# Two of eight tile pairs of a final weighted sum computed by GpSimd instead of VectorE

## What is computed

```python
x = x + 0.5 * ffn(layernorm(x))      # first expert layer
x = x + attention(layernorm(x))
x = x + 0.5 * ffn(layernorm(x))      # second expert layer

# in ffn: each token goes to the best 4 of 16 experts
vals, idx = top_k(logits, 4)
gates_k = softmax(vals)
y = einsum('emi,edi->emd', act, w2) + b2
delta = einsum('me,emd->md', G, y)   # G holds the 4 gates of a token
return x + delta
```

## Time and profile before

| | us |
|---|---|
| median of 3 runs | 1039.29 |
| lowest, highest | 1039.18, 1043.13 |
| the profiled execution | 1044.55 |
| its span | 1042.8 |
| its last stage, from the last indirect DMA at 1003.98 | 38.8 |

### The profile page before, as it was taken

One profiled execution on the slowest core, in us unless ns is written; L12 is line 12 of the kernel. 1 busy time (PEld: TensorE's weight loads), 2 busy tenths in 40 slices (PEclk: granted clock), 3 DMA queues, 4 the chain that ended last, 5 costly groups with the idle time before them and its releaser, 6 DMA issues.

```text
span 1042.8 us, 22336 instructions
## 1 busy us (share of the span) xinstructions
PE 712.3 (68%) x5722; PEld 427.6 (41%) x5722; DVE 610.4 (59%) x1961; ACT 445.8 (43%) x974; POOL 328.5 (32%) x356
## 2 busy tenths in 40 slices
PE   2222079999999926767788297287209999999930
PEld 1111046555665613223343143144106666666620
DVE  6776335555555555677787268237405566666547
ACT  2533035555555524336556135142005555555520
POOL 3667613333333313101111500503532333333320
PEclk9999999999999977869999699698559999999985
DMA  9654334555445344622212313325232333333338
GB/s 306 252 207 160 121 104 130 167 167 164 149 126 138 89 134 129 199 73 72 79 32 59 122 39 101 118 83 180 105 119 82 90 92 95 95 92 94 85 121 282
DMA packets 120111, 131.63 MB, mean 126 GB/s; under 512 B 39596, under 2 KB 101525, under 8 KB 119864
## 3 DMA queue, kind: packets, MB, share of 16 engines
q1 hardware_dynamic: 101656, 91.11, 29.3%
q0 software_dynamic: 13728, 34.64, 9.3%
q10 hardware_dynamic: 4608, 4.46, 1.2%
HBM read 69.54 MB, written 64.21 MB: 128 GB/s over the span
## 4 chain that ended last, share of the span: by engine, by line
PE 46%; DVE 12%; issue 11%; SPq 10%; ACT 7%; another core or an unknown queue 5%; DMA 4%; ACTq 4%; POOL 0%; DVEq 0%; POOLq 0%
PE banks L406 15%; PE banks L428 7%; ACT w2s L1438 4%; PE banks L1233 3%; PE banks L415 3%; PE banks L388 2%; PE banks L402 2%; PE banks L1278 2%; PE banks L1211 2%; SPq L218 2%; DVE X L726 2%; DVE X L1545 2%; SPq L231 2%; SPq L217 2%
## 5 line engine op out<-in xcount | busy, mean ns | idle before, releaser
L340 POOL DMA_INDIRECT y_rows<-y,goal x158 | 155.4, 984 | 333.5 <-ACT y L498 318.4
L406 PE MATMUL banks<-w1s,rT 128*128 x948 | 233.7, 383 | 0.0
L688 DVE TENSOR_SCALAR pbh<-banks 128x256 f32<-128x256 f32 x158 | 67.1, 425 | 199.7 <-ACT pbh L484 128.7
L1603 DVE CUSTOM_DVE_ANT_0 pbh<-banks,maskq 128x128 bf16<-128x128 f32 (+3 forms) x256 | 113.2, 487 | 69.8 <-PE banks L1188 46.3
L1438 ACT ACTIVATE w2s<-banks 128x1024 f32<-128x1024 f32 (+3 forms) x128 | 89.6, 700 | 138.1 <-PE banks L1219 98.6
L406 PEld LDWEIGHTS banks<-w1s,rT 128*128 128x128 f16 x948 | 93.6, 99 | 96.4 <-issue 4.0
L428 PE MATMUL banks<-w2s,hsT 128*128 x948 | 129.2, 273 | 0.0
L484 ACT ACTIVATE pbh<-banks 128x256 f32<-128x256 f32 x158 | 60.5, 383 | 125.2 <-PE banks L406 118.6
L477 ACT ACTIVATE rT<-banks 128x512 f16<-128x512 f16 x158 | 93.5, 592 | 42.7 <-issue 35.5
L1125 POOL DMA_INDIRECT x_rows<-row,row_to x64 | 61.8, 965 | 132.0 <-DVE row_to L1736 113.7
L491 ACT ACTIVATE hsT<-pbh 128x256 f16<-128x256 f32 x158 | 65.8, 416 | 72.1 <-DVE pbh L696 49.2
(11 more groups left out here) (238 smaller groups left out, 1077.9 us busy)
## 6 DMA issues: line engine op xcount, KB each, us to landing
row<-x_rows SPq DMA_DIRECT2D x158, 128.0 KB
arena<-in_w SPq DMA_DIRECT2D x16, 512.0 KB, 7.5
w1s<-y_rows SPq DMA_DIRECT2D x16, 512.0 KB, 5.0
arena<-y_rows SPq DMA_DIRECT2D x16, 512.0 KB, 7.8
qk_split<-w1s SPq DMA_DIRECT2D x48, 128.0 KB
arena<-qk_split SPq DMA_DIRECT2D x64, 96.0 KB, 2.3
w_lent<-w1s SPq DMA_DIRECT2D x22, 256.0 KB
w1s<-w_lent SPq DMA_DIRECT2D x11, 512.0 KB
```

What stands on the lines that cost most here:

```text
L340: pool.indirect_dma_start(y_rows[m], bass.IndirectOffsetOnAxis(ap=goal[:, c, :], axis=0), y[:, n % NY, :], None, bounds_check=K * T - 1, o ...
L406: mm = pe.matmul(o, rT[:, n % 2, 2 * r + k, :], w1s[:, bass.ds(e, 1), k, w, :], start=False, stop=(k == HC - 1 and w == 1))
L1603: dve.tensor_tensor_reduce(junk[:, (n * U + j) % 3, 0:W], query_bank[j % 4][:, 0:W], maskq[:, SEQ - W:], 1.0, -3e38, ALU.add, ALU.max, mx[ ...
```

## The change

Pairs 2 and 5 are summed by GpSimd. [...] Each addition waits for its multiplication. The semaphore `pool_summed` counts these instructions, 16 for a pair. They stand in GpSimd's program behind the last indirect DMA. VectorE sums pairs 0, 1, 3, 4, 6 and 7. The semaphore `combined` goes; SyncE waits for the count of sums of whichever engine has the pair. SyncE's order of loads and stores stays.

```diff
+            BY_POOL = (2, 5)
+            BY_DVE = tuple(j for j in range(NT // 2) if j not in BY_POOL)
...
+                def wait_combined(j):
+                    if j in BY_POOL:
+                        sp.wait_ge(ev("pool_summed"), (BY_POOL.index(j) + 1) * K * 2 * 2)
+                    else:
+                        sp.wait_ge(ev("summed"), (BY_DVE.index(j) + 1) * K * 2)
...
                 def store_out(j):
-                    sp.wait_ge(ev("combined"), j + 1)
+                    wait_combined(j)
...
                         if i >= NB:
-                            sp.wait_ge(ev("combined"), (i - NB) // 2 + 1)
+                            wait_combined((i - NB) // 2)
                         load_back(i)
...
+                for j in BY_POOL if m == 1 else ():
+                    for k in range(K):
+                        for t in range(2):
+                            i, done = 2 * j + t, BY_POOL.index(j) * K * 2 + 2 * k + t
+                            if k == 0:
+                                pool.wait_ge(y_back[i % NB], i // NB * 16 + 16)
+                            pool.tensor_scalar(back[:, i % NB, k, :], back[:, i % NB, k, :], gate[:, i, k:k + 1], None,
+                                               ALU.mult).then_inc(ev("pool_summed"), 1)
+                            pool.wait_ge(ev("pool_summed"), 2 * done + 1)
+                            if k == 0:
+                                pool.wait_ge(ev("residual"), i + 1)
+                            pool.tensor_tensor(X[:, i, :], X[:, i, :], back[:, i % NB, k, :], ALU.add)\
+                                .then_inc(ev("pool_summed"), 1)
...
-                                dve.wait_ge(ev("summed"), (j * K + k - 1) * 2 + t + 1)
+                                dve.wait_ge(ev("summed"), (BY_DVE.index(j) * K + k - 1) * 2 + t + 1)
...
-                    dve.wait_ge(ev("summed"), (j + 1) * K * 2)
-                    dve.sem_inc(ev("combined"), 1)
...
-                for j in range(NT // 2 if m == 1 else 0):
+                for j in BY_DVE if m == 1 else ():
                     combine(j)
```

## The result

The changed kernel takes 1053.64 us (median of 4 runs, 1048.99 to 1057.25) against 1039.24 us: a ratio of 1.0133, 95% interval 1.0077 to 1.0190. A second series gave 1.0117 (1.0070 to 1.0164). It is slower, as forecast, but by 14 us where 5.7 were forecast, and it lies above the range, whose top was 1052.

What follows compares the result with a forecast made beforehand. The prediction took VectorE's sums to bound the last stage, with the loads 0.5 us behind. VectorE's end 5.4 us later plus 0.3 us of stores gave +5.7 us on the median 1039.29, so 1045.0 us; range 1040.5 to 1052.

Steps and rivals of the forecast that it cites:

- The bound and what could be had: Last stage: VectorE ends last, loads close behind; of 8.1 us taken off VectorE at most 0.5 to 0.8 reach the end.
- the slack: Last token tile's load: said to land at 1035.0, wanted by VectorE at 1035.45, so 0.5 us to spare.
- The exclusion: VectorE's sums and GpSimd's instructions reading SBUF wait for each other; 10.6 us put on VectorE for 8.1 taken off.
- unit: One GpSimd multiplication and the addition waiting for it, 16 in all: 1.29 us alone, 1.67 us beside VectorE.
- the same rule: VectorE loses the length of the GpSimd instruction less 0.26 us: 0.47 to an addition, 0.19 to a multiplication.
- The multiplication: GpSimd's multiplication by a pointer scalar, not in the trace: taken as 0.45 us, between 0.30 and 0.73.
- SyncE's queue: Loads 12 and 13 wait for GpSimd's pair 2, with later loads and stores behind them; out about 8 us later.
- The timetable: Last stage event by event: GpSimd's pair 2 ends at 1029.5, pair 5 at 1042.9, VectorE at 1044.1, 5.4 us later.
- Rival 3: Longer GpSimd units: 1.95 us gives +9.7 (1049), 1.98 gives +11.2 (1050.5), both together +15 us; chance 0.17.
- The sum: Whole change: VectorE ends 5.4 us later, the bunched last stores add 0.3, together +5.7 us.

Runs made afterwards that it cites:

- fills: The changed kernel with GpSimd's multiplications and additions replaced by as many fills of the same tiles; last stage 36.1 us, one run.
- no_pool: The changed kernel with no pair on GpSimd: VectorE sums all eight, SyncE waits for the sums directly; last stage 35.2 us, 1.0014 of the kernel before.
- own_buffers: The changed kernel with 16 load buffers instead of 8, so that no load waits for a pair; last stage 50.4 us, 1.0179 of the kernel before.
- drain_first: The changed kernel with an added GpSimd drain right behind the last indirect DMA; last stage 45.3 us, 1.0099 of the kernel before.

## Why the prediction was wrong, point by point

- **The bound and what could be had: right in kind.** VectorE alone bounded the last stage, with the loads close behind. The gain was capped by the loads: 48 undisturbed sums (fills) ended as late as 64 without the handshake (no_pool), 31.1 us. The cap was 1.5 us and not 0.5 to 0.8, in part because the slack was read at the first sum of pair 7 and not at tile 15's.
- **The exclusion: right, and what VectorE loses to the size.** Forecast: VectorE loses 0.47 us to an addition and 0.19 to a multiplication, 0.66 a unit, and gets a sum through per 0.66 us. Measured: 0.94 - 0.48 = 0.46, 0.69 - 0.48 = 0.21, 0.67 a unit, a sum per 0.63 us. GpSimd does not lose 0.19 us to each of its two, as I had it, but 0.17 to the multiplication and nothing to the addition. That 0.19 for the multiplication came near 0.21 is luck: it was 0.45 - 0.26, and the same rule with the measured 0.92 would give 0.66. The Trainium skill, in the section that the prediction names ("SBUF — State Buffer", "Who interferes with whom"), has its words on the whole instruction with VectorE's two-port modes; of two SBUF inputs it says that they contend, and here they cost 0.46 of an addition's 0.72 us.
- **The multiplication: the term of the sum that was mis-sized.** 0.45 us taken, 0.30 and 0.73 as bounds; measured 0.92 alone, 1.09 beside VectorE, above both. The bounds came from a fill, a select and an addition, none of which was of this form. That a unit is 1.88 or 1.71 us, not far from the forecast 1.67, is again luck: the gap before the addition is 0.09 us and not 0.16, and GpSimd loses 0.17 a unit and not 0.38, which hides 0.28 of the 0.47 that the multiplication was short. The first multiplication took 2.24 us. GpSimd's chain of 16 units took 30.5 us instead of 26.8, and ended 40.4 us into the stage instead of 36.7 (1042.9): 3.7 us.
- **SyncE's queue: right as a mechanism, wrong as the cause.** Loads 12 and 13 went out 10.7 us late (forecast 8) and VectorE idled. But GpSimd's chain ended as late as VectorE; own_buffers took the wait away, and the last store landed no sooner than in drain_first, which has it (43.5 and 43.4 us). The timetable put VectorE's end 1.2 us behind GpSimd's and so made it look decisive.
- **The drain: the step that was missing**, 5.0 us, a term put at nothing without a reason. The prediction took the 4.1 us between VectorE's end and the end of the span as fixed, and asked only who waits for sums. The indirect DMA of line 340 is not GpSimd's last instruction: its queue held a drain of 10.5 us from 1003.2 on, visible in the trace and hidden because the engine had been done for 34 us. Rival 3 had the long units (chance 0.17), and its +9.7 is near the 9.3 without the drain, but not this.
- **The sum.** Forecast: 5.4 of sums + 0.3 of stores = 5.7. Measured: 9.3 until the last store has landed (40.7 - 32.5 = 8.2 of sums, 1.1 of stores, three of which now stand behind each other) + 5.0 of drain = 14.3. Without the drain it is 9.3, inside the range. With the forecast's own end of GpSimd's chain, the drain alone makes the stage 36.7 + 8.8 + 1.7 (from the drain's end to the span's) = 47.2 us, +10.5: so of the 8.6 us that the forecast was short, 4.8 are the drain and 3.8 the longer chain.

## What to carry to other kernels

Before work is given to an engine that had been idle at the end, look at what stands last in its queue: a wait that was hidden there (here 8.8 us) moves to wherever its last instruction now is. GpSimd is no spare VectorE for tensors in SBUF: its reading instructions hold up VectorE's sums, which have two SBUF inputs, by 0.46 us for an addition and 0.21 for a multiplication, 0.67 us a unit here against the 0.40 us that the unit takes off VectorE. A relief is worth no more than what bounds next, here the loads: look for that bound at the instruction that needs the last tile. And the price of an instruction form that the trace doesn't show need not be bounded by a neighbouring form, even one that reads more (0.92 us here, above the 0.73 of an addition).

## What the runs showed of the hardware

- GpSimd's multiplication of 128x256 float32 by a scalar: 0.92 us with the scalar from SBUF, 0.85 with a constant; as a product of two tensors 0.61 us alone and 0.79 beside VectorE; the addition 0.72.
- The first drain of GpSimd in this kernel ended 8.8 us after the end of the instruction ahead of it in every trace, whether that was an indirect DMA, an addition or a fill, and also 33.7 us after the last indirect DMA; a second one ended 0.07 us after it. The drain's rows are 8.9 to 10.5 us long, and 0.8 and 1.7 for a second one, because they start sooner.
- GpSimd fills (0.31 us each) left VectorE's sums at 0.48 us; GpSimd's additions made them 0.94, its multiplications 0.69.
